# Attention over columns on one core: score blocks from the diagonal on, x transposed from a second layout, factors summed by DMAs

## The chip, the core and the metric

The kernel runs on one core of a Trainium2 chip. The engines that matter here are TensorE (PE, with its weight loads shown apart as PEld), VectorE (DVE), ScalarE (ACT), GpSimd (POOL) and the queues that issue DMAs (SP for all DMAs of the kernel before). The metric is the device time of one execution in microseconds (us); lower is better.

## The reference

Four blocks follow each other on `x` of 8 x 512 x 512 float32 values. Only the first is touched by the change, and the sum of `factors` that the second one uses:

```python
def _L0_attn_ref(x):
    scores = jnp.einsum('bci,bcj->bij', x, x)
    weights = jax.nn.softmax(scores, axis=-1)
    context = jnp.einsum('bij,bcj->bci', weights, x)
    return context
...
x = L0_attn_x
x = x + _layernorm(_L0_attn_ref(_layernorm(x, axis=-1)), axis=-1)
x = x + _layernorm(_L0_ffn_ref(_layernorm(x, axis=-1), L0_ffn_factors, L0_ffn_bias), axis=-1)
```

In the first block each batch's scores are a 512 x 512 matrix that is symmetric, because it is the product of `x` transposed with `x`. The second block multiplies `x` by the sum of eight 512 x 512 factors. Two more blocks (grouped attention, gated FFN) follow.

## The kernel before

`four_blocks` calls one function per block; each ends with all engines meeting, and then the next begins. The change is in `column_attention`. A batch is 4 tiles of 128 rows by 512 columns (`T` = 4, `N` = 512, `P` = 128), and the eight batches `b` are worked on one after the other, with `p` = 0 or 1 as the half of each doubled buffer. Every engine has its own program, and semaphores tie them together; the order in which each engine works is the order in which its program is written.

For one batch the steps are these.

- SP loads `x` of the next batch and one factor.
- DVE takes the statistics of the four tiles (`stats_of`), POOL turns them into scales (`scales_of`, four short instructions of 4 columns), DVE normalises (`xn`, L335) and rounds to the float32r type (`xh`, L341), and POOL forms the rest (`xl` = `xn` - `xh`, L231). A product of two float32 matrices is made of three float32r products: high by high, low by high, high by low.
- PE, `scores` of tile t (S0 to S3 below): 12 matmuls of 128x512 into one PSUM bank of two. Behind each S, `turn` makes 4 transposes of `xn` (128x128 each) into one of two banks `turned`. ACT copies them to `xth` (L292), DVE forms `xtl` (L357).
- DVE takes the row maximum (L345), ACT the exponential into `prob` (L282), DVE the inverse of the sum, POOL multiplies (L236). PE turns `prob` (4 transposes per tile), ACT and DVE make `pth` and `ptl` from it in the same way.
- PE, `contexts` of tile t (C0 to C3): again 12 matmuls of 128x512, for the batch before. DVE takes their statistics, POOL makes the scales, ACT normalises (`normed`, L301), and POOL adds to `x` (L247), one batch later still.
- DVE adds the factor that was loaded to `factor_sum` (L391, 128x2048).

The loops over batches are real loops on the engines except for the first and last batches (`over_batches`, `over_batches_two_behind`). `following.statistics` and `following.row_scales` already do the statistics of batch 0 for the second block.

## Time and profile before

| | us |
|---|---|
| median of three runs | 1650.66 (1650.22 to 1652.57) |
| the profiled execution's own time | 1653.88 |
| its span, from first to last instruction | 1652.0 |
| stage in question: start to the second block's first matmul | 257.05 |

The profile is of one execution. A row names the line, the engine, the instruction with what it writes and reads, and its shape; times of groups are sums, and a mean in nanoseconds. In the timeline the first number is the start in us from the start of the span, the second the length; a count such as x4 behind the shapes says how many instructions were merged into the row; a bracket says how long the engine was idle before it, and what ended that. Matmuls are pipelined, so the time that one costs is the distance between two starts.

### The profile page before, as it was taken

How to read it: one execution, taken by the hardware profiler on the slowest of the kernel's cores; microseconds unless marked ns; L12 is line 12 of the kernel's file. 1: busy time of each engine (PE TensorE's matmuls, PEld its weight loads, DVE VectorE, ACT ScalarE, POOL GpSimd, SP SyncE). 2: the span in 40 equal slices, each digit the busy share in tenths (PEclk: the TensorE clock that was granted, in tenths of full speed). 3: DMA queues.
4: the chain of work that ended last, by engine and by line, in shares of the span. 5: the costliest groups of instructions: out<-in, count | busy, mean ns of one | idle time of the engine just before them, and what ended most of it. 6: DMA issues, size and time to landing. Idle time of an engine off the chain costs nothing.

```text
span 1652.0 us, 22026 instructions
## 1 busy us (share of the span) xinstructions
PE 1498.8 (91%) x7332; PEld 1214.2 (73%) x7332; DVE 1048.3 (63%) x2091; ACT 789.7 (48%) x1506; POOL 733.4 (44%) x914
## 2 busy tenths in 40 slices
PE   4999996995899999999999998579899999999996
PEld 3777775874687877778787876467688888888885
DVE  4698846874888888888888778545424334234233
ACT  1333334644877878687878777321212222222121
POOL 3486742663444545454545445213243333333331
PEclk9999997997999999999999999889999999999998
DMA  4121102224000202020202020222110110100100
GB/s 152 52 102 51 50 1 71 76 89 141 1 1 1 77 1 77 2 77 1 77 1 77 1 96 1 83 96 90 33 51 1 51 51 0 51 32 18 51 26 26
DMA packets 41797, 80.00 MB, mean 48 GB/s; under 512 B 2416, under 2 KB 3440, under 8 KB 41712
## 3 DMA queue, kind: packets, MB, share of 16 engines
q1 hardware_dynamic: 41712, 78.93, 13.7%
q8 instruction: 46, 0.75, 0.2%
q14 instruction: 39, 0.32, 0.1%
HBM read 53.75 MB, written 25.17 MB: 48 GB/s over the span
## 4 chain that ended last, share of the span: by engine, by line
PE 57%; DVE 10%; POOL 4%; issue 3%; ACT 3%; DMA 1%; SPq 0%; POOLq 0%; DVEq 0%; ACTq 0%
PE f_inner L57 22%; PE g_side L1381 12%; PE f_down L1792 9%; PE g_score L57 5%; PE g_turned L1401 5%; DVE g_ptl L1305 2%; PE g_output L1427 2%; PE g_output L1429 2%; DVE g_neg_max L1291 2%; DVE f_wl L1716 1%; POOL g_prob L1016 1%; PE f_inner L1764 1%; POOL g_power L990 1%; DVE g_q L1220 1%; ACT g_pth L1167 1%
## 5 line engine op out<-in xcount | busy, mean ns | idle before, releaser
L1016 POOL TENSOR_SCALAR g_prob<-g_prob,g_inv_sum 128x512 f32<-128x512 f32 x256 | 178.7, 698 | 308.4 <-DVE g_inv_sum L1296 308.4
L57 PE MATMUL f_inner<-f_xth,f_wh 128*128 128x512 f32 x704 | 281.3, 400 | 15.8 <-DVE f_wl L1716 12.7
L57 PE MATMUL f_inner<-f_xtl,f_wh 128*128 128x512 f32 x704 | 279.5, 397 | 0.0
L1685 DVE SCALAR_TENSOR_TENSOR f_hidden<-f_inner,f_inner_scale,f_silu 128x512 f32<-128x512 f32 x88 | 66.0, 750 | 313.8 <-PE f_inner L57 313.8
L1574 POOL TENSOR_TENSOR f_hl<-f_hidden,f_hh 128x512 fp32r<-128x512 f32 x88 | 128.1, 1456 | 296.8 <-DVE f_hh L1691 296.8
L1626 ACT ACTIVATE f_silu<-f_inner,f_inner_scale 128x512 f32<-128x512 f32 x88 | 60.7, 690 | 413.8 <-PE f_inner L57 413.8
L1291 DVE TENSOR_REDUCE g_neg_max<-g_score 128x1 f32<-128x512 f32 x256 | 175.4, 685 | 83.9 <-PE g_score L57 82.7
L1125 ACT ACTIVATE g_prob<-g_score,g_neg_max 128x512 f32<-128x512 f32 x256 | 177.0, 691 | 96.9 <-DVE g_neg_max L1291 94.7
L1305 DVE TENSOR_TENSOR g_ptl<-g_turned,g_pth 128x512 fp32r<-128x512 f32 x256 | 173.8, 679 | 15.6 <-ACT g_pth L1167 13.6
L1401 PE MATMUL g_turned<-identity,g_prob 128*128 128x128 f32 x1024 | 155.2, 274 | 27.1 <-DVE g_ptl L1305 27.0
L57 PEld LDWEIGHTS f_inner<-f_xth,f_wh 128*128 128x128 f32 x704 | 133.1, 189 | 54.6 <-DVE f_wl L1716 17.5
L1167 ACT CAST g_pth<-g_turned 128x512 fp32r<-128x512 f32 x256 | 149.5, 584 | 46.7 <-PE g_turned L1401 44.6
L1401 PEld LDWEIGHTS g_turned<-identity,g_prob 128*128 128x128 f32 x1024 | 121.3, 140 | 64.3 <-issue 34.4
L57 PEld LDWEIGHTS f_inner<-f_xtl,f_wh 128*128 128x128 f32 x704 | 133.2, 189 | 31.7
L1792 PE MATMUL f_down<-f_wh,f_hh 128*128 128x512 f32 x352 | 140.1, 398 | 0.9 <-POOL f_hl L1574 0.9
L1792 PE MATMUL f_down<-f_wh,f_hl 128*128 128x512 f32 x352 | 139.3, 396 | 0.0
L57 PE MATMUL g_score<-g_kh,g_q 128*128 128x512 f32 x256 | 122.2, 478 | 2.7 <-DVE g_q L1220 2.7
L1427 PE MATMUL g_output<-g_pth,g_v 128*128 128x512 f32 x256 | 101.0, 395 | 1.6 <-DVE g_ptl L1305 1.6
L57 PE MATMUL g_score<-g_kl,g_q 128*128 128x512 f32 x256 | 100.9, 394 | 0.0
L1429 PE MATMUL g_output<-g_ptl,g_v 128*128 128x512 f32 x256 | 100.6, 393 | 0.0
L1792 PEld LDWEIGHTS f_down<-f_wh,f_hh 128*128 128x128 f32 x352 | 66.3, 188 | 16.9 <-POOL f_hl L1574 1.3
L1792 PEld LDWEIGHTS f_down<-f_wh,f_hl 128*128 128x128 f32 x352 | 66.4, 189 | 15.5
(200 smaller groups left out, 3460.3 us busy)
## 6 DMA issues: line engine op xcount, KB each, us to landing
x_resident<-x SPq DMA_DIRECT2D x8, 1024.0 KB, 7.0
x_mixed<-x_resident SPq DMA_DIRECT2D x8, 1024.0 KB, 4.4
x_pair<-x_mixed SPq DMA_DIRECT2D x8, 1024.0 KB, 7.8
g_res<-x_mixed SPq DMA_DIRECT2D x8, 1024.0 KB, 6.1
x_attended<-g_res SPq DMA_DIRECT2D x8, 1024.0 KB, 5.1
x_pair<-x_attended SPq DMA_DIRECT2D x8, 1024.0 KB, 5.7
factor<-factors SPq DMA_DIRECT2D x7, 1024.0 KB, 5.2
out<-x_pair SPq DMA_DIRECT2D x7, 1024.0 KB, 4.3
```

Of the source, the lines that this page charges most:

```text
L57: last = nc.tensor.matmul(out, lhsT, rhs, start=(n == 0), stop=(n == len(pairs) - 1))
L1016: nc.gpsimd.tensor_scalar(prob[:, at, :], prob[:, at, :], inv_sum[:, at:at + 1], 1.0, ALU.mult, ALU.mult).then_inc(prob_ready, 1)
L1125: nc.scalar.activation(prob[:, at, :], score[u % 2][:, :], ACT.Exp, bias=neg_max[:, at:at + 1], scale=1.0, accum_out=row_sum[:, at:at + 1] ...
L1167: nc.scalar.copy(pth[:, (turn_u // T) % 2, :, at * P:(at + 1) * P], blocks_of(turned[turn_u % 2][:, :])).then_inc(hi_ready, 1)
L1291: nc.vector.reduce_max(neg_max[:, at:at + 1], score[u % 2][:, :], AX, negate=True).then_inc(max_ready, 1)
L1305: nc.vector.tensor_tensor(ptl[:, at, :, cols], blocks_of(turned[turn_u % 2][:, :]), pth[:, at, :, cols].bitcast(F32), ALU.subtract).then_i ...
L1381: last = nc.tensor.matmul(out[:, bank_cols], *pairs[n], start=(k == 0 and n == 0), stop=(k == T - 1 and n == 2))
L1401: mm = nc.tensor.transpose(turned[turn_u % 2][:, cols], prob[:, turn_u % 4, cols], s.identity[:, :])
L1427: nc.tensor.matmul(output[hd % 2][:, :], lhsT, pth[:, hd % 2, t, :], start=(t == 0), stop=False)
L1429: mm = nc.tensor.matmul(output[hd % 2][:, :], lhsT, ptl[:, hd % 2, t, :], start=False, stop=(t == T - 1))
L1574: nc.gpsimd.tensor_tensor(hl[:, at, :], hidden[:, at, :], hh[:, at, :].bitcast(F32), ALU.subtract).then_inc(hl_ready, 1)
L1792: last = nc.tensor.matmul(down[t][:, :], l[:, at, cols], r[:, i, 2, :], start=(i == 0 and n == 0), stop=(i == IT - 1 and n == len(halves) ...
```

## The change

What it does, step by step.

- **Scores.** Tile t multiplies only the columns from block t on: 12 matmuls of 512, 384, 256 and 128 columns for t = 0 to 3. ACT copies the blocks right of the diagonal out of PSUM into `upper` (`copy_upper`), and PE transposes them into the place of the blocks left of it in the later tiles (1, 2 and 3 transposes for t = 1, 2, 3). The row maximum waits for the copy.
- **x transposed.** It is no longer turned on PE. The host gives `x_t`, the transpose of the raw `x`, as a further input; SP loads it in two halves per batch into `xt`, ACT makes `xth` and DVE `xtl` from SBUF. It is not normalised: since the rows of the weights sum to one, the context of the raw `x` differs from that of the normalised one by a scale and a shift per row, which the layernorm behind takes out. POOL computes the epsilon that goes with it (`raw_eps`, one more instruction per batch).
- **Normalising.** `xn` moves from DVE to POOL, `xh` from DVE to ACT (straight from `x`), `xl` from POOL to DVE.
- **Factors.** Factor 0 is loaded as before. Factors 1 to 7 are added to `factor_sum` in SBUF by DMAs with an add, issued from POOL, each behind a wait for the one before; the DVE instruction L391 goes. At the end of the stage POOL waits for the last one.
- **Output.** The output statistics and scales are made for two tiles at a time (`output_stats`, `output_scales(b, h)`, four instructions per half), `normed` has four buffers, and PE's order is new. All programs of the stage are written out for eight batches, with no loop left.

The core of the diff; the parts removed are in the functions above, and "..." marks what is left out.

```diff
+    def load_x(b):
+        sp.dma_start(s.x[:, b * T:(b + 1) * T, :], rows_of(x_in, b)).then_inc(x_loaded, 16)
+
+    def load_half(b, h):
+        if b > 0:
+            sp.wait_ge(xtl_ready, (b - 1) * T + 2 * h + 2)
+        sp.dma_start(xt[:, 2 * h:2 * h + 2, :],
+                     rows_of(xt_in, b)[:, 2 * h:2 * h + 2, :]).then_inc(xt_loaded[h], 16)
+
+    load_x(0)
+    for b in range(B):
+        if b < B - 1:
+            sp.wait_ge(x_loaded, b * 16 + 16)
+            load_x(b + 1)
+        for h in range(2):
+            load_half(b, h)
+        if b == 0:
+            sp.dma_start(s.factor_sum[:, :, :], rows_of(factors, 0)).then_inc(factor_loaded, 16)
...
     def scales_of(b):
...
+        nc.gpsimd.tensor_scalar(raw_eps[:, b % T, :], mv[:, :, 1], EPS, EPS, ALU.add, ALU.mult)
...
+            nc.gpsimd.tensor_scalar(xn[:, t, :], s.x[:, b * T + t, :], mv[:, t, 0:1], rs[:, t:t + 1],
+                                    ALU.subtract, ALU.mult).then_inc(xn_ready, 1)
...
+        nc.gpsimd.tensor_tensor(ove[:, half], omv[:, half, 1], raw_eps[:, b % T, half], ALU.add)
...
+    def add_factor(b):
+        if b == 1:
+            pool.wait_ge(factor_loaded, 16)
+        else:
+            pool.wait_ge(factor_summed, (b - 1) * 16)
+        nc.gpsimd.dma_start(s.factor_sum[:, :, :], rows_of(factors, b),
+                            accum_op=ALU.add).then_inc(factor_summed, 16)
...
+    normalised(0, range(T))
...
+    def body(b, p, first, last):
+        if b >= 2:
+            add(b - 2, 0)
+            output_scales(b - 2, 1)
+            add(b - 2, 1)
+            add(b - 2, 2)
+        probabilities(b, p, 0)
+        if last:
+            following.row_scales(nc, s, pool)
+        else:
+            scales_of(b + 1)
+        probabilities(b, p, 1)
         if not last:
-            for t in range(T):
-                lo_of(b + 1, 1 - p, t)
-
-    over_batches_two_behind(pool, body)
-    output_scales(B - 2)
-    for t in range(T):
+            normalised(b + 1, (0, 1, 2))
+        probabilities(b, p, 2)
+        if not last:
+            normalised(b + 1, (3,))
+        if not first:
+            output_scales(b - 1, 0)
+        probabilities(b, p, 3)
+        if b >= 2:
+            add(b - 2, 3)
+        if not first:
+            add_factor(b)
...
+        nc.scalar.activation(xh[:, p, t, :], s.x[:, b * T + t, :], ACT.Identity, bias=shift[:, t:t + 1],
+                             scale=rs[:, t:t + 1]).then_inc(xh_ready, 1)
...
+    def copy_upper(b, t):
+        act.wait_ge(scored, b * T + t + 1)
+        nc.scalar.copy(upper[t][:, :], score[t % 2][:, (t + 1) * P:]).then_inc(copied, 1)
...
+        nc.scalar.copy(xth[:, p, t, :], xt[:, t, :]).then_inc(xth_ready, 1)
...
+    def body(b, p, first, last):
+        hi_of_xt(b, p, 0)
+        hi_of_xt(b, p, 1)
+        copy_upper(b, 0)
+        if not first:
+            hi_of_prob(b - 1, 1 - p, 2)
+            hi_of_prob(b - 1, 1 - p, 3)
+        if b >= 2:
+            norm(b - 2, 2)
+        exp(b, p, 0)
+        copy_upper(b, 1)
+        if b >= 2:
+            norm(b - 2, 3)
+        exp(b, p, 1)
+        copy_upper(b, 2)
+        if not last:
+            hi_of_xn(b + 1, 1 - p, 0)
+        exp(b, p, 2)
+        if not last:
+            hi_of_xn(b + 1, 1 - p, 1)
+        hi_of_prob(b, p, 0)
+        if not last:
+            hi_of_xn(b + 1, 1 - p, 2)
+        hi_of_prob(b, p, 1)
+        exp(b, p, 3)
+        if not last:
+            hi_of_xn(b + 1, 1 - p, 3)
+        if not first:
+            norm(b - 1, 0)
+            norm(b - 1, 1)
+        hi_of_xt(b, p, 2)
+        hi_of_xt(b, p, 3)
...
+    def lo_of_xn(b, p, t):
+        dve.wait_ge(xn_ready, b * T + t + 1)
+        dve.wait_ge(xh_ready, b * T + t + 1)
+        nc.vector.tensor_tensor(xl[:, p, t, :], xn[:, t, :], xh[:, p, t, :].bitcast(F32),
+                                ALU.subtract).then_inc(xl_ready, 1)
...
+        nc.vector.tensor_tensor(xtl[:, p, t, :], xt[:, t, :], xth[:, p, t, :].bitcast(F32),
+                                ALU.subtract).then_inc(xtl_ready, 1)
 
     def maximum(b, p, t):
         dve.wait_ge(scored, b * T + t + 1)
+        if t < T - 1:
+            dve.wait_ge(copied, b * (T - 1) + t + 1)
...
     def body(b, p, first, last):
+        if b >= 2:
+            output_stats(b - 2, 3)
         if not last:
...
+            tile_stats(b + 1, 0)
+            tile_stats(b + 1, 1)
+            tile_stats(b + 1, 2)
+        maximum(b, p, 0)
+        if not first:
+            lo_of_prob(b - 1, 1 - p, 2)
+            lo_of_prob(b - 1, 1 - p, 3)
+        if not last:
+            tile_stats(b + 1, 3)
+            stats_of(b + 1)
+        if last:
+            dve.wait_ge(added, T)
+            following.statistics(nc, dve, [s.x[:, t, :] for t in range(T)])
+        inverse(b, p, 0)
+        maximum(b, p, 1)
+        lo_of_xt(b, p, 0)
+        if not first:
+            output_stats(b - 1, 0)
+        inverse(b, p, 1)
+        lo_of_xt(b, p, 1)
+        maximum(b, p, 2)
+        if not last:
+            lo_of_xn(b + 1, 1 - p, 0)
+        inverse(b, p, 2)
+        if not last:
+            lo_of_xn(b + 1, 1 - p, 1)
+        if not first:
+            output_stats(b - 1, 1)
+        lo_of_prob(b, p, 0)
+        maximum(b, p, 3)
+        lo_of_prob(b, p, 1)
+        if not last:
+            lo_of_xn(b + 1, 1 - p, 2)
+        inverse(b, p, 3)
+        if not last:
+            lo_of_xn(b + 1, 1 - p, 3)
+        if not first:
+            output_stats(b - 1, 2)
+        lo_of_xt(b, p, 2)
+        lo_of_xt(b, p, 3)
...
+        if t > 0:
+            pe.wait_ge(copied, b * (T - 1) + t)
+        for r in range(t):
+            nc.tensor.transpose(score[t % 2][:, block_at(r)], upper[r][:, block_at(t - r - 1)],
+                                s.identity[:, :])
+        products(nc, score[t % 2][:, t * P:],
+                 [(l[:, p, k, block_at(t)], r[:, p, k, t * P:])
                   for k in range(T) for l, r in ((xh, xh), (xl, xh), (xh, xl))]).then_inc(scored, 1)
...
     def body(b, p, first, last):
+        scores(b, p, 0, first)
+        if not first:
+            turn(b - 1, 1 - p, 2, b == 1)
+            turn(b - 1, 1 - p, 3, b == 1)
+        scores(b, p, 1, first)
+        if not first:
+            contexts(b - 1, 1 - p, 0)
+        scores(b, p, 2, first)
+        if not first:
+            contexts(b - 1, 1 - p, 1)
+        turn(b, p, 0, first)
+        scores(b, p, 3, first)
+        turn(b, p, 1, first)
+        if not first:
+            contexts(b - 1, 1 - p, 2)
+        if last:
+            turn(b, p, 2, first)
+            turn(b, p, 3, first)
+        if not first:
+            contexts(b - 1, 1 - p, 3)
+
```

PE's program, before, in the steady state: behind the 12 matmuls of S (`score`) stand four transposes of `xn`.

```order
L57 MATMUL score<-xl,xh 128x512
L57 MATMUL score<-xh 128x512
L57 MATMUL score<-xh,xl 128x512
L57 MATMUL score<-xl,xh 128x512
L439 MATMUL turned<-identity,xn 128x128 x4
```

PE's program now, around S3 (the fourth score tile): the turn of `prob`'s tile 0, the three blocks turned from copies, and the first of 12 narrow matmuls.

```order
L57 MATMUL context<-ptl,xth 128x512
L543 MATMUL turned<-identity,prob 128x128 x4
L532 MATMUL score<-identity,upper 128x128 x3
L57 MATMUL score<-xh 128x128
L57 MATMUL score<-xh,xl 128x128
L57 MATMUL score<-xl,xh 128x128
```

The four transposes of `xn` behind each score tile are gone, `turn` serves `prob` alone, and the matmuls of this tile are a quarter as wide.

DVE's program before, in the steady state, from the factor on (REGISTER_ALU is the loop's bookkeeping).

```order
L391 TENSOR_TENSOR factor_sum<-factor_sum,factor 128x2048
L350 RECIPROCAL inv_sum<-row_sum 128x1
L344 REGISTER_ALU
L345 TENSOR_REDUCE neg_max<-score 128x1
L354 REGISTER_ALU
L357 TENSOR_TENSOR xtl<-turned,xth 128x4x128
L335 TENSOR_SCALAR xn<-x_resident,mv,rs 128x512 x2
L350 RECIPROCAL inv_sum<-row_sum 128x1
```

DVE's program now, from the last two tiles of `xtl` of one batch to the work that C0 of that batch waits for (`ptl` of `prob`'s tiles 2 and 3).

```order
L441 BN_STATS obn<-context 128x6
L419 TENSOR_TENSOR xtl<-xt,xth 128x512 x2
L441 BN_STATS obn<-context 128x6
L449 BN_AGGR omv<-obn 128x2 x2
L398 BN_STATS bn<-x_resident 128x6 x3
L426 TENSOR_REDUCE neg_max<-score 128x1
L436 TENSOR_TENSOR ptl<-turned,pth 128x4x128 x2
L398 BN_STATS bn<-x_resident 128x6
```

The factor's addition, `xn` and `xh` have left DVE; `xl` and `xtl` now both read two tiles in SBUF, and nine instructions stand ahead of `ptl`'s last two tiles.

POOL's program now, steady state, from the last step of one batch to the scales of the next but one.

```order
L243 TENSOR_SCALAR prob<-prob,inv_sum 128x512
L259 TENSOR_TENSOR x_resident<-x_resident,normed 128x512
L266 DMA factor_sum<-factors 128x4x512
L259 TENSOR_TENSOR x_resident<-x_resident,normed 128x512
L249 TENSOR_TENSOR ove<-omv,raw_eps 128x2
L250 TENSOR_SCALAR oshift<-omv 128x2
L252 TENSOR_TENSOR ors<-ove,minus_half 128x2
L254 TENSOR_TENSOR oshift<-oshift,ors 128x2
L259 TENSOR_TENSOR x_resident<-x_resident,normed 128x512 x2
L243 TENSOR_SCALAR prob<-prob,inv_sum 128x512
```

Before, POOL had no DMA, and in the place of the four `xn` that it has now (L238) stood the four `xl` (L231). The DMA stands ahead of the second half of the output scales, behind which ACT's program has `norm` and then `exp` of the next batch.

## Rows read from the trace of the kernel before

**Rows 1.** The page of the profile: span, and busy time of each engine.

```profile
span 1652.0 us, 22026 instructions
...
PE 1498.8 (91%) x7332; PEld 1214.2 (73%) x7332; DVE 1048.3 (63%) x2091; ACT 789.7 (48%) x1506; POOL 733.4 (44%) x914
```

**Rows 2.** Windows: busy us (xcount) per engine, granted clock, DMA share, GB/s.

```profile
19.30:44.50 25.20, 18.89 (x80) 15.13 (x80) 14.18 (x32) 7.41 (x16) 10.49 (x12) 0.89 0.24 84
44.50:71.00 26.50, 26.44 (x120) 21.64 (x121) 17.75 (x35) 7.13 (x15) 12.62 (x12) 0.91 0.22 80
```

**Rows 3.** Timeline of PE, steady state, one group of twelve matmuls.

```profile
111.97 0.48 PE L57 MATMUL context<-pth,xth 128*128 128x512 f32 x1
112.29 0.39 PE L57 MATMUL context<-pth,xtl 128*128 128x512 f32 x1
...
114.59 0.39 PE L57 MATMUL context<-ptl,xth 128*128 128x512 f32 x1
115.18 0.48 PE L57 MATMUL context<-pth,xth 128*128 128x512 f32 x1
```

**Rows 4.** Timeline of PE in grouped attention: float32r matmuls of 128 columns.

```profile
398.04 0.28 PE L1381 MATMUL g_side<-g_wvl,g_hth 128*128 128x128 f32 x1
...
399.94 0.28 PE L1381 MATMUL g_side<-g_wvh,g_htl 128*128 128x128 f32 x1
```

**Rows 5.** Timeline of DVE: the factor's addition in two batches.

```profile
108.09 2.28 DVE L391 TENSOR_TENSOR factor_sum<-factor_sum,factor 128x2048 f32<-128x2048 f32 x1
...
134.81 2.28 DVE L391 TENSOR_TENSOR factor_sum<-factor_sum,factor 128x2048 f32<-128x2048 f32 x1
```

**Rows 6.** Timeline of POOL beside it, and the same instruction later.

```profile
107.19 0.70 POOL L236 TENSOR_SCALAR prob<-prob,inv_sum 128x512 f32<-128x512 f32 x1 [5.07 <-DVE inv_sum L350]
...
108.27 2.18 POOL L104 TENSOR_SCALAR shift<-mv 128x4 f32<-128x4 f32 x1
...
127.20 0.23 POOL L104 TENSOR_SCALAR oshift<-omv 128x4 f32<-128x4 f32 x1
```

**Rows 7.** Waits of 40 to 260 us: total, times, longest.

```profile
PE turned L439 <- DVE ptl L357: 5.1, 6, 2.3
```

**Rows 8.** Timeline of the stage's start, all engines.

```profile
7.88 0.50 SPq L212 DMA_DIRECT2D factor_sum<-factors  x1
...
10.41 0.24 POOL L103 TENSOR_SCALAR ve<-mv 128x4 f32<-128x4 f32 x1 [8.84 <-DVE mv L328]
...
12.38 1.91 DVE L335 TENSOR_SCALAR xn<-x_resident,mv,rs 128x512 f32<-128x512 f32 x4 [2.07 <-POOL shift L108]
...
14.71 4.47 POOL L231 TENSOR_TENSOR xl<-xn,xh 128x512 fp32r<-128x512 f32 x2 [2.36 <-DVE xh L341]
...
19.28 0.76 PE L57 MATMUL score<-xh 128*128 128x512 f32 x1 [19.28 <-POOL xl L231]
...
24.54 1.05 PE L439 MATMUL turned<-identity,xn 128*128 128x128 f32 x4
...
44.56 0.79 PE L57 MATMUL score<-xh 128*128 128x512 f32 x1 [3.03 <-POOL xl L231]
```

**Rows 9.** Groups by line, 70 to 202 us.

```profile
L247 POOL TENSOR_TENSOR x_resident<-x_resident,normed 128x512 f32 (+1 forms) x20 | 28.3, 1415 | 0.0
...
L357 DVE TENSOR_TENSOR xtl<-turned,xth 128x512 fp32r<-128x512 f32 x20 | 13.6, 682 | 2.1 <-ACT xth L292 2.1
...
L292 ACT CAST xth<-turned 128x512 fp32r<-128x512 f32 x20 | 11.7, 585 | 20.5 <-PE turned L439 20.4
```

**Rows 10.** The page's DMA issues: count, KB each, us to landing.

```profile
factor<-factors SPq DMA_DIRECT2D x7, 1024.0 KB, 5.2
```

**Rows 11.** Timeline of the stage's end.

```profile
248.50 0.39 PE L57 MATMUL context<-ptl,xth 128*128 128x512 f32 x1
...
252.09 2.99 ACT L301 ACTIVATE normed<-context,oshift,ors 128x512 f32<-128x512 f32 x4 [13.51 <-POOL oshift L108]
...
257.05 1.33 PE L695 MATMUL turned<-identity,xn 128*128 128x128 f32 x5 [8.16 <-ACT xn L574]
```

More of the change, by code:

```diff
@@ L159, in column_attention @@
         prob = sb("prob", [P, T, N])
-        normed = sb("normed", [P, 2, N])
-        factor = sb("factor", [P, T, N])
+        upper = [sb(f"upper{t}", [P, N - (t + 1) * P]) for t in range(T - 1)]
+        normed = sb("normed", [P, 4, N])
         bn = sb("bn", [P, T, 6])
@@ L244, in add @@
-            def add(b, t):
-                pool.wait_ge(ctx_normed, b * T + t + 1 + T)
-                x = tile_of(s.x, b * T + t)
-                nc.gpsimd.tensor_tensor(x, x, normed[:, t % 2, :], ALU.add).then_inc(added, 1)
-            scales_of(0)
-            for t in range(T // 2):
-                lo_of(0, 0, t)
-            pool.sem_inc(xl_ready, T // 2)
-            def body(b, p, before, last):
-                if before == 2:
-                    output_scales(b - 2)
-                for t in range(T):
-                    normalise(b, p, t)
-                    if t == 0 and not last:
-                        scales_of(b + 1)
-                    if before == 2:
-                        add(b - 2, t)
-                if not last:
-                    for t in range(T):
-                        lo_of(b + 1, 1 - p, t)
@@ L304, in body, with hi_of_xt @@
[L304 to L316 removed]
+            def hi_of_xt(b, p, t):
+                if t % 2 == 0:
+                    act.wait_ge(xt_loaded[t // 2], b * 16 + 16)
+                if t == 0 and b >= 2:
+                    act.wait_ge(ctx_ready, (b - 1) * T)
+                nc.scalar.copy(xth[:, p, t, :], xt[:, t, :]).then_inc(xth_ready, 1)
@@ new lines, in hi_of_prob @@
+            def hi_of_prob(b, p, g):
+                act.wait_ge(turn_ready, b * T + g + 1)
+                nc.scalar.copy(pth[:, p, :, block_at(g)], blocks_of(turned[g % 2][:, :])).then_inc(hi_ready, 1)
+            def norm(b, t):
+                act.wait_ge(oscales, b * 2 + t // 2 + 1)
+                if b == B - 1 and t >= 4:
+                    act.wait_ge(last_added, t - 4 + 1)
+                elif b * T + t >= 4:
+                    act.wait_ge(added, b * T + t - 4 + 1)
+                nc.scalar.activation(normed[:, t % 4, :], context[t][:, :], ACT.Identity,
+                                     bias=oshift[:, t:t + 1], scale=ors[:, t:t + 1]).then_inc(ctx_normed, 1)
@@ L360, in output_stats, with lo_of_prob @@
-            def output_stats(b, t):
-                dve.wait_ge(ctx_ready, (b + 1) * T + t + 1)
-                last = nc.vector.bn_stats(obn[:, t, :], context[t][:, :])
-                if t == T - 1:
-                    last.then_inc(own_obn, 1)
-                    wait_alone(dve, s, own_obn, b + 1)
-                    for t in range(T):
+            def lo_of_prob(b, p, g):
+                dve.wait_ge(hi_ready, b * T + g + 1)
+                nc.vector.tensor_tensor(ptl[:, p, :, block_at(g)], blocks_of(turned[g % 2][:, :]),
+                                        pth[:, p, :, block_at(g)].bitcast(F32), ALU.subtract).then_inc(lo_ready, 1)
@@ L403, in _ @@
-            over_batches(dve, body)
-            dve.wait_ge(added, T + 2)
-            following.statistics(nc, dve, [s.x[:, t, :] for t in range(T)])
-            for t in range(T):
-                output_stats(B - 1, t)
-            for t in range(T):
-                dve.wait_ge(ctx_normed, B * T + t + 1)
-                x = tile_of(s.x, (B - 1) * T + t)
-                nc.vector.tensor_tensor(x, x, normed[:, t % 2, :], ALU.add).then_inc(last_added, 1)
+            for t in range(T):
+                tile_stats(0, t)
@@ new lines, in add_last @@
+            def add_last(t):
+                dve.wait_ge(ctx_normed, (B - 1) * T + t + 1)
+                x = s.x[:, (B - 1) * T + t, :]
+                nc.vector.tensor_tensor(x, x, normed[:, t % 4, :], ALU.add).then_inc(last_added, 1)
+            written_out(body)
+            output_stats(B - 2, 3)
+            for t in range(T - 1):
+                output_stats(B - 1, t)
+            add_last(0)
+            add_last(1)
+            output_stats(B - 1, 3)
+            add_last(2)
+            add_last(3)
```

241 lines of the change are left out of this document (97 added, 144 removed).

## The prediction

> **What bounds the stage now.** The page comes first: PE is busy 91% of a span of 1652.0 us [rows 1]. The change touches only what lies ahead of the second block's first matmul, 257.05 us [rows 11]; the rest I take as unchanged. The timeline of PE in the steady state shows starts of 128x512 matmuls 0.230 us apart (10 steps in 2.30 us), and a group of twelve with its four transposes 3.21 us [rows 3]. A batch has eight such groups, 25.7 us. The factor's addition, once per batch, comes back after 26.72 us [rows 5], so PE stands about 1.0 us per batch. The waits name the reason for most of it: `turned` waits for DVE's `ptl`, 5.1 us in 6 times [rows 7]. So PE sets the period of the batches. At both ends it does not: the first matmul starts at 19.28 us behind a chain of DMA, statistics, scales, `xn`, `xh`, `xl`, and batch 1 starts at 44.56 us, after PE has stood for POOL's `xl` [rows 8].
>
> **PE's sum per batch.** A float32r matmul of 128 columns costs 0.112 us (17 steps in 1.90 us) where its columns alone would be a quarter of 0.230, so below some width the cost is flat [rows 4]. No row has 384 or 256 columns. Bounds: by columns 0.172 and 0.115, from above 0.230 each. I take the columns, since 512 columns go by them nearly (0.213 at the full level of 2.4 GHz) and 0.115 is just over the flat cost of [rows 4]. Twelve each: S0 2.76, S1 2.07, S2 1.38, S3 1.34, together 7.55 us in place of 11.0. A group's four transposes cost 3.21 - 12 x 0.230 = 0.45 with the change over to them and back [rows 3], so `prob`'s four turns cost 1.8, and the six blocks of `upper`, in three groups, 1.0 (bounds 0.7 to 1.35). Contexts stay at 11.0. Sum 21.35 us, against 25.7: 3.5 less by narrower scores, 1.8 less by `xn`'s turns, 1.0 more by `upper`. With both unseen widths at their upper bound it would be 12 x (0.058 + 0.115) = 2.1 more.
>
> **What is moved, and whether it hides.** ACT gets 4 passes from SBUF for `xh` (0.75 each as L301 [rows 11]) and three short copies, below 0.585 each [rows 9]; at 20 passes of at most 0.8 and 4 row sums it stays under 18 us. DVE loses the factor (2.28), `xn` and `xh` and gets `xl`: 24 passes of 0.68 [rows 9], about 16.5 us, and some 1.5 of small ones. POOL is the one to watch. Scales: the four small instructions take from 10.41 to 12.38, 1.97 us [rows 8]; with `raw_eps` 2.3. Two halves of output scales 3.9. Four adds at 1.415 [rows 9], 5.7. Four `prob` and four `xn` of 0.70 [rows 6] (`xn` at most as an add), 5.6. That is 17.5 us. The DMA's issue, D, is in no row of POOL: below it 0 (SP's takes 0.50 and hides [rows 8]), above it four passes of 1.415, 5.7, since it names 2048 columns. I take 1.5, nearer to the SP row. On top come holds. While DVE added the factor, two tiles in SBUF, a POOL instruction of 0.23 us took 2.18 [rows 5, 6]: DVE instructions of that kind stop POOL. That was 2.28 us per batch and is now `xl` and `xtl`, 8 x 0.68 = 5.4. So POOL needs 17.5 to 17.5 + 5.4 + 1.5 = 24.4, and with D at its bound 28.6. The holds cost only where POOL has work at that moment; its program waits for `prob` tiles in four places, so I count half: 21.7, close behind PE.
>
> The Trainium skill, "SBUF — State Buffer", section "SBUF: two separate sides", says that the pair of ports is locked for a whole instruction by whichever of the two engines comes first, so that DVE would also wait for POOL. The trace shows only POOL waiting, while DVE takes its 2.28 us each time [rows 5, 6]; what the other direction would give is the second rival. By the Trainium skill, "DMA: Bandwidth & Descriptors", section "Latency and other measured facts", the start of a DMA from POOL costs about 1 us; with that the sum above would be 0.5 us per batch shorter, and no run here shows it.
>
> **The loop behind C0.** PE order makes a second ring: C0, S2, C1, turn, S3, turn take 2.76 + 1.8 + 2.76 + 0.45 + 1.8 + 0.45 = 10.0; from there ACT must do `pth`, `exp`, `xh`, two `normed` and two `xth`, 4.9 at 0.585 to 0.8, then DVE the last `xtl`, output statistics, three statistics of the next batch, the maximum and `ptl` twice, 8 x 0.68 + 0.4 = 5.8. That is 20.7, before the next C0 may start: shorter than PE's 21.35 by 0.6, so two holds are enough to make it the bound. I therefore keep the 1.0 us per batch of standing that [rows 3, 5] give for before: **period 22.35 us** in place of 26.72.
>
> **The start.** Scales end 0.3 later than 12.38 [rows 8]. Then POOL makes four `xn` (2.8) and DVE four `xl` (2.7), ACT's `xh` beside them; one after the other at worst, so S0 starts at 18.2 (15.9 if they overlap wholly) for 19.28. POOL's two `xl` of 4.47 us are gone. S0 runs at the low clock level as now, 5.26 us [rows 8], to 23.5. S1, partly at the low level, with its copy: 27.1. Maximum, `exp` and S2, S3: about 31. Batch 1's four `xn` and `xl` come behind POOL's `prob` 1 at 30.0: 5.5 more, so batch 1 starts at 35.5 for 44.56 (34 to 38). PE stands some 4 us before, as it did for 3.0 us; then the 26.5 us after 44.5 had a mean clock of 0.91, which cost 2.4 us [rows 2], and I keep that.
>
> **Sum.** 35.5 + 2.4 + 7 x 22.35 (156.5) + 0.9 (two turns of batch 7 within its own body) + 11.0 (last contexts) + the end. The end runs from 248.73 to 257.05, 8.3 us [rows 11]; ACT's four `normed` in a row (2.99) become two, and the statistics of half the tiles are done: 6.6. Sum 212.9, that is 44.2 us less than 257.05. The profiled execution took 1653.88, its span 1652.0, the median 1650.66; the gain comes off each: 1609.7 and, for the median, 1606.5. One step of 1 us in the period is 7 us.
>
> Costed at nothing: 8 MB more of loads. Per batch 3 MB, in 22 us, for 2 MB now; a 1 MB DMA lands in 5.2 us [rows 10]. Their cover is a batch's period, and without it each half of `xt` would hold ACT. The DMA that adds must land within a period, or POOL waits in front of the next; below 22 us it costs nothing, and the last is issued some 20 us before the stage ends. The written out programs cost nothing, as the first batch and the last are that already.
>
> **Rivals.**
> - POOL binds. All holds count and D is 1.5 to 5.7: period 24.4 to 28.6, typically 25. For it: 8 holds for one. Against it: POOL is idle at several waits. It gives 1606.5 + 7 x 2.65 = 1625. Chance 0.25.
> - DVE is held by POOL too. Eight instructions wait half an instruction of 0.7 to 1.4, 0.5 us each; five of them lie in the ring behind C0 or what feeds it: 20.7 + 2.5 = 23.2, so 1612. It is the mechanism of the rule of the Trainium skill ("SBUF — State Buffer") above. Chance 0.2.
> - Narrow matmuls cost more than their columns, up to 2.1 per batch: at most 1621, more likely 1612. [rows 4] speak against a great excess. Chance 0.07.
> - Slower than before: the DMA with its addition (issue on POOL or landing) takes longer than a period. The wait in `add_factor` then stands in front of POOL's next `x` add, output scales, ACT's `normed` and `exp`. It decides from a period of 22.35 + 44.2/7 = 28.7 us; at 30 us it gives 1660. A plain DMA lands in 5.2 [rows 10]. Chance 0.04.
> - The forecast, period 21.35 to 23, 1599 to 1611: chance 0.41. The last 0.03 is for a better start and PE without any standing, below 1599.
>
> **Numbers.** The likeliest is 1606. The range holds the first three rivals in their usual sizes: 1596 (period 21.35, batch 1 at 34 and S0 at 16) to 1628 (period 25.4). What can be told from no change is 0.2%, 3.3 us. Faster needs a period below 28.2: all cases but the slow one and the far end of the first rival. Faster 0.94, within 0.2% 0.02, slower 0.04.
>
> **What the profile after would show.** PE: distances of 0.172, 0.115 and 0.112 us within S1, S2, S3; a period (from S0 to S0) of 22.35; first matmul near 18, batch 1 at 35.5; the second block's first matmul at 213. POOL: if its idle time in the steady state is near nothing, and PE waits for `xl`, `turned` or `context` with POOL behind, the first rival holds; if `xl` and `xtl` of DVE take over 0.68, the second; if `x_resident` on POOL waits for a DMA, the slow one. I would be wrong above all through D and through how many holds hit.

## The result, and the profile after

The changed kernel took 1661.13 us (median of four runs, 1659.48 to 1663.25), the kernel before 1650.62 beside it (1650.22 to 1652.57). The ratio is 1.0062, with a 95% interval of 1.0045 to 1.0079: slower by 0.6%, where 1606 was forecast. Run again later, the ratio was 1.0052 (1.0034 to 1.0069).

The page of the changed kernel first, beside [rows 1]:

```profile
span 1657.7 us, 21618 instructions
...
PE 1470.7 (89%) x7252; PEld 1196.0 (72%) x7252; DVE 1023.0 (62%) x2050; ACT 818.5 (49%) x1562; POOL 774.5 (47%) x963
```

PE's busy time is 28 us less, and the span is longer. So PE waits more. POOL is busy 41 us more than before. One line of its code stands out: 32 `xn` take 78 us, 2.45 in the mean, where 0.70 each, as I had counted, gives 22. This is the answer for line 238 of the changed kernel, `xn` on POOL (min, median and max in ns):

```profile
L238 POOL TENSOR_SCALAR xn<-x_resident,mv,rs x32: 2066/2600/2613, 12.5 to 211.2; 128x512 f32<-128x512 f32 x32
...
who waited for it (us, times):
  DVE xl L414: 44.5, 25
```

The prediction has 0.70 us for it. The start shows what that does, against [rows 8] (timelines of the changed kernel):

```profile
12.50 9.86 POOL L238 TENSOR_SCALAR xn<-x_resident,mv,rs 128x512 f32<-128x512 f32 x4
...
23.23 0.77 PE L57 MATMUL score<-xh 128*128 128x512 f32 x1 [23.23 <-DVE xl L414]
...
46.11 0.77 PE L57 MATMUL score<-xh 128*128 128x512 f32 x1 [9.64 <-issue]
```

Four `xn` take 9.86 us where 2.8 was counted; S0 starts at 23.23 (19.28 before) and batch 1 at 46.11 (44.56 before). In the steady state a batch looks like this on PE, POOL and ACT (timelines, from one S0 to the next):

```profile
98.40 0.47 PE L57 MATMUL score<-xh 128*128 128x512 f32 x1 [0.18 <-issue]
...
109.70 0.75 PE L57 MATMUL context<-pth,xth 128*128 128x512 f32 x1 [3.75 <-issue]
...
127.59 0.47 PE L57 MATMUL score<-xh 128*128 128x512 f32 x1 [0.88 <-issue]
```

```profile
116.23 7.28 POOL L238 TENSOR_SCALAR xn<-x_resident,mv,rs 128x512 f32<-128x512 f32 x3
123.50 0.68 POOL L243 TENSOR_SCALAR prob<-prob,inv_sum 128x512 f32<-128x512 f32 x1
124.17 2.60 POOL L238 TENSOR_SCALAR xn<-x_resident,mv,rs 128x512 f32<-128x512 f32 x1
126.74 0.19 POOL L249 TENSOR_TENSOR ove<-omv,raw_eps 128x2 f32<-128x2 f32 x1
```

```profile
128.71 1.45 ACT L345 ACTIVATE normed<-context,oshift,ors 128x512 f32<-128x512 f32 x2 [3.48 <-POOL oshift L254]
```

This period is 29.19 us, against 26.72 in [rows 5]; over the steady state of this trace a batch takes 27.8 to 29.2. Read from POOL on: `prob` of tile 2 stands behind three `xn` (DVE had its `inv_sum` at 119.13, and `prob` starts at 123.50), the output scales behind the fourth (`omv` was there at 122.54, and they start at 126.74). ACT waits 3.48 us for those scales, and its `xth` stand behind `normed`. In DVE's program the last `xtl` waits for `xth`, and behind it stand statistics, a maximum and the last two `ptl`, without a gap. PE's first context group needs `xtl` and `ptl`; the `ptl` come last, and end where its wait of 3.75 us ends:

```profile
108.33 1.28 DVE L436 TENSOR_TENSOR ptl<-turned,pth 128x512 fp32r<-128x512 f32 x2
```

This is the ring of "The loop behind C0" in the prediction, with POOL's `xn` now in front of ACT's `normed`. The wait costs PE once more: in the stretch behind it (109.70 to 112.81) the granted clock is 0.50, the lower of its two levels (1.2 GHz), and the matmuls of this group start 0.43 us apart for 0.23. That is 1.7 us of the period. The windows put POOL's sum beside it:

```profile
98.40:127.59 29.19, 23.30 (x118) 19.46 (x119) 18.53 (x37) 13.97 (x27) 24.48 (x26) 0.94 0.41 108
```

POOL is busy 24.48 us of the period. My sum of 17.5 with 2.45 in place of 0.70 for each of four `xn` gives 24.5. The issue of the DMA (1.35 us) is not in that column; with it POOL has 25.8 us of work.

The prediction also asked whether DVE is held by POOL. It is. In the same timeline:

```profile
101.35 1.35 POOL L266 DMA_DIRECT2D factor_sum<-factors  x1
101.50 3.67 DVE L419 TENSOR_TENSOR xtl<-xt,xth 128x512 fp32r<-128x512 f32 x2 [2.59 <-ACT xth L333]
102.26 1.74 POOL L259 TENSOR_TENSOR x_resident<-x_resident,normed 128x512 f32<-128x512 f32 x1
```

Two `xtl` take 3.67 us, where two of 0.68 each would take 1.4. How much of that is the add's and how much the DMA's, the kernels without the DMA show below.

### The profile page after: what moved, and what is told of

Read it like the earlier page. It is cut to its first block, busy times and chain, and to the rows that moved or that the text cites. A ratio compares the mean times of both kernels' runs of the same rounds, so it can differ in the third digit from the quotient of the medians.

```text
span 1657.7 us, 21618 instructions
## 1 busy us (share of the span) xinstructions
PE 1470.7 (89%) x7252; PEld 1196.0 (72%) x7252; DVE 1023.0 (62%) x2050; ACT 818.5 (49%) x1562; POOL 774.5 (47%) x963
## 3 DMA queue, kind: packets, MB, share of 16 engines
q1 hardware_dynamic: 42368, 79.98, 13.9%
## 4 chain that ended last, share of the span: by engine, by line
PE 59%; DVE 10%; POOL 3%; issue 3%; ACT 2%; DMA 1%; SPq 0%; POOLq 0%; DVEq 0%; ACTq 0%
PE f_inner L57 22%; PE g_side L1497 13%; PE f_down L1908 9%; PE g_score L57 5%; PE g_turned L1517 5%; PE g_output L1543 2%; PE g_output L1545 2%; DVE g_ptl L1421 2%; DVE g_neg_max L1407 2%; DVE f_wl L1832 1%; DVE g_q L1336 1%; PE f_inner L1880 1%; POOL g_prob L1132 1%; DVE f_hidden L1801 1%; POOL g_power L1106 1%
## 5 line engine op out<-in xcount | busy, mean ns | idle before, releaser
L1421 DVE TENSOR_TENSOR g_ptl<-g_turned,g_pth 128x512 fp32r<-128x512 f32 x256 | 173.6, 678 | 15.5 <-ACT g_pth L1283 13.5
L57 PE MATMUL score<-xh 128*128 128x512 f32 (+3 forms) x128 | 45.6, 356 | 37.5 <-DVE xl L414 23.2
```

What stands on the lines that cost most here:

```text
L57: last = nc.tensor.matmul(out, lhsT, rhs, start=(n == 0), stop=(n == len(pairs) - 1))
L1421: nc.vector.tensor_tensor(ptl[:, at, :, cols], blocks_of(turned[turn_u % 2][:, :]), pth[:, at, :, cols].bitcast(F32), ALU.subtract).then_i ...
```

## The experiments

The theory: the form of POOL's `xn`, that is the pair of operations it is written with, costs the forecast gain. The main rival: the DMA that adds does, by its issue on POOL and by what it holds on DVE. A smaller question is which of the forecast's other terms stand once the first is mended.

The runs were made in three groups, each beside the kernel before, with medians of 1651.87, 1652.19 and 1652.5 us (1650.62 beside the result). So a difference of times between two groups is uncertain by one or two us; where it matters, the stage's time in the traces stands beside it. "The stage" is the time from the start of the span to the second block's first matmul: 257.05 before, 259.24 in the changed kernel.

### The form of POOL's `xn`, alone

```diff
-nc.gpsimd.tensor_scalar(xn[:, t, :], s.x[:, b * T + t, :], mv[:, t, 0:1], rs[:, t:t + 1],
-                        ALU.subtract, ALU.mult).then_inc(xn_ready, 1)
+nc.gpsimd.tensor_scalar(xn[:, t, :], s.x[:, b * T + t, :], rs[:, t:t + 1], shift[:, t:t + 1],
+                        ALU.mult, ALU.add).then_inc(xn_ready, 1)
```

> The changed kernel, with one edit: POOL's xn is x * rs + shift (multiply, add) instead of (x - mean) * rs (subtract, multiply). Theory A, the form of POOL's xn is the cause: in the changed kernel these 32 instructions took 2.45 us each, while grouped attention's instruction of the same shape with two column operands and multiply, add (g_xn) took 0.77. xn then takes about 0.77, a batch loses up to 4 x 1.68 = 6.7 us of the 29.2 us from S0 to S0, down to about 22.5 us, batch 1 starts some 13 us earlier than 46 us, and the median is near 1661 - 47 - 13 = 1601 us, at least below 1615. Theory B, the port that DVE and POOL share and the DMA's issue are the cause, xn's 2.45 us being mostly time held back: xn stays above 1.5 us and the median above 1640 us.

Measured: 1611.57 us (1609.64 to 1612.66), ratio 0.9749 (0.9736 to 0.9763). That is 49.6 us less than the changed kernel, by one line that computes the same function from `shift`, which POOL had made already; the stage ends at 210.17 for 259.24. It is within theory A's bound of 1615, though 10 us above its likeliest 1601, and theory B (above 1640) falls. Line 238 and the start in its trace:

```profile
L238 POOL TENSOR_SCALAR xn<-x_resident,rs,shift x32: 760/768/1312, 12.6 to 163.1; 128x512 f32<-128x512 f32 x32
```

```profile
12.64 4.59 POOL L238 TENSOR_SCALAR xn<-x_resident,rs,shift 128x512 f32<-128x512 f32 x4
...
18.11 0.76 PE L57 MATMUL score<-xh 128*128 128x512 f32 x1 [18.11 <-DVE xl L414]
...
36.84 0.77 PE L57 MATMUL score<-xh 128*128 128x512 f32 x1 [5.31 <-issue]
```

```profile
100.00:122.00 22.00, 21.09 (x119) 18.25 (x118) 19.44 (x37) 14.01 (x28) 18.22 (x27) 1.00 0.57 144
```

The period is 22.15 us (DVE's statistics of a batch start at 83.89, 106.04 and 128.19), PE is busy 21.09 of 22 us, POOL 18.22 without the DMA's issue, and the granted clock is 1.00. This is the kernel that the prediction describes.

### `xn` back on DVE

```diff
+            def xn_of(b, t):
+                if t == 0:
+                    dve.wait_ge(scales, b + 1)
...
+                nc.vector.tensor_scalar(xn[:, t, :], s.x[:, b * T + t, :], mv[:, t, 0:1], rs[:, t:t + 1],
+                                        ALU.subtract, ALU.mult).then_inc(xn_ready, 1)
+
             def lo_of_xn(b, p, t):
+                xn_of(b, t)
```

> The changed kernel, with xn given back to DVE, directly ahead of each xl; POOL has no xn. Theory A: POOL loses 4 x 2.45 us per batch and is no bound any more; DVE gains 4 x 0.5 to 1.2 us and is near 21 us per batch, so the period is 22 to 24 us and the median 1600 to 1618 us. Theory B: with xn gone from POOL the instructions held back are others, and the median stays above 1635 us.

`normalised` and its calls on POOL are gone (not shown). Measured: 1613.87 us (1612.91 to 1615.44), ratio 0.9763 (0.9748 to 0.9778), with a period of 22.92, as theory A has it. The same subtraction and multiplication takes DVE 0.533 us, so it is dear on POOL and not on DVE, and either cure gives the gain.

### Four forms in one kernel

```diff
+                    dst, src, m, r = xn[:, t, :], s.x[:, b * T + t, :], mv[:, t, 0:1], rs[:, t:t + 1]
+                    if t == 0:
+                        done = nc.gpsimd.tensor_scalar(dst, src, m, r, ALU.subtract, ALU.mult)
+                    elif t == 1:
+                        done = nc.gpsimd.tensor_scalar(dst, src, m, r, ALU.add, ALU.mult)
+                    elif t == 2:
+                        done = nc.gpsimd.tensor_scalar(dst, src, r, m, ALU.mult, ALU.subtract)
+                    else:
+                        done = nc.gpsimd.tensor_scalar(dst, src, r, m, ALU.mult, ALU.add)
```

> The changed kernel, with POOL's xn in four forms, one for each tile, same operands in shape and place: subtract, multiply; add, multiply; multiply, subtract; multiply, add. The values of xn are then not those of the reference in three of four tiles. Theory A says that the duration goes with the pair of operations, and this run says with which part of it: if subtraction is what is slow, tiles 0 and 2 take 2.0 to 2.6 us and the others 0.77; if it is any pair that doesn't begin with a multiplication, tiles 0 and 1; if only multiply, add is fast, tiles 0, 1 and 2. Theory B, time held back by DVE: all four alike, since the same DVE work stands beside them.

The values of three tiles in four are not the reference's here; only durations are read. Measured: 1645.13 us in the one run, period 27.5. The first batch (timeline of POOL and DVE; a form per line):

```profile
12.66 2.09 POOL L240 TENSOR_SCALAR xn<-x_resident,mv,rs 128x512 f32<-128x512 f32 x1
14.74 1.30 POOL L242 TENSOR_SCALAR xn<-x_resident,mv,rs 128x512 f32<-128x512 f32 x1
14.79 0.69 DVE L422 TENSOR_TENSOR xl<-xn,xh 128x512 fp32r<-128x512 f32 x1 [4.43 <-POOL xn L240]
...
16.03 2.62 POOL L244 TENSOR_SCALAR xn<-x_resident,rs,mv 128x512 f32<-128x512 f32 x1
...
18.63 1.30 POOL L246 TENSOR_SCALAR xn<-x_resident,rs,mv 128x512 f32<-128x512 f32 x1
```

The forms with a subtraction cost 2.09 and 2.62 us, those with an addition 1.30: not all four alike, so theory B falls here too. Tiles 1 to 3 run while DVE forms the `xl` of the tile before (14.79), and are held by it: 0.76 alone against 1.30 beside an `xl`, and 2.07 against 2.60 in the changed kernel, are the same 0.53 us. That the `xl` is what holds them is read from their standing side by side. Freed of it, a subtraction costs 2.07, an addition 0.76, in either place of the pair.

### Four more forms

```diff
+                    if t == 0:
+                        done = nc.gpsimd.tensor_scalar(dst, src, m, None, ALU.subtract)
+                    elif t == 1:
+                        done = nc.gpsimd.tensor_scalar(dst, src, 0.5, 2.0, ALU.subtract, ALU.mult)
+                    elif t == 2:
+                        done = nc.gpsimd.tensor_scalar(dst, src, m, None, ALU.add)
+                    else:
+                        done = nc.gpsimd.tensor_scalar(dst, src, 0.5, 2.0, ALU.add, ALU.mult)
```

> The changed kernel with xn of the four tiles in four other forms on lines of their own, which change the values of xn: tile 0 subtracts a column and does no more, tile 1 subtracts 0.5 and multiplies by 2, tile 2 adds a column and does no more, tile 3 adds 0.5 and multiplies by 2. Theory A (a subtraction of a scalar operand is what is slow on POOL): tiles 0 and 1 at least 2.0 us when not held, tiles 2 and 3 below 0.8. Rival 1 (two operations with two different column operands are slow when one is a subtraction): tile 1 is fast, 0.7 to 0.8. Rival 2 (it is slow only with two operations): tile 0 is fast. No theory of the whole time; two slow tiles would give about 1645, four fast ones 1612.

Here too the kernel computes other values. Measured: 1622.09 us in the one run. The lines are tiles 0 to 3 in this order, with min, median and max in ns:

```profile
L240 POOL TENSOR_SCALAR xn<-x_resident,mv x8: 1568/1576/1587, 12.4 to 171.4; 128x512 f32<-128x512 f32 x8
L242 POOL TENSOR_SCALAR xn<-x_resident x8: 1924/1932/1935, 13.9 to 173.0; 128x512 f32<-128x512 f32 x8
L244 POOL TENSOR_SCALAR xn<-x_resident,mv x8: 1573/1579/2112, 15.9 to 174.9; 128x512 f32<-128x512 f32 x8
L246 POOL TENSOR_SCALAR xn<-x_resident x8: 613/618/627, 17.9 to 177.1; 128x512 f32<-128x512 f32 x8
```

Subtracting 0.5 and multiplying by 2 takes 1.93 us, adding 0.5 and multiplying by 2 takes 0.62: rival 1 falls, the columns are not the reason. Subtracting a column and doing no more takes 1.58, so rival 2 falls. But adding a column and doing no more takes 1.58 us, as long as subtracting it, so theory A is too narrow as well: it held for tiles 0, 1 and 3 only up to its number (1.58 for "at least 2.0") and not for tile 2. What these rows bear out is that POOL has a few cheap pairs (multiply with multiply, add with multiply, multiply with add: 0.62 to 0.77 us) and that what is outside them costs 1.6 to 2.1. Why stays open.

### One slow tile in four

The kernel with the cheap form, but tile 3 subtracts and multiplies as in the change.

```diff
+                    if t == 3:
+                        nc.gpsimd.tensor_scalar(xn[:, t, :], s.x[:, b * T + t, :], mv[:, t, 0:1], rs[:, t:t + 1],
+                                                ALU.subtract, ALU.mult).then_inc(xn_ready, 1)
```

> The kernel e1_mult_add with the xn of one tile in four (tile 3) in the form of the changed kernel, subtraction and multiplication. POOL is busy 18.2 of 22 us per batch in e1, and gets 1.3 to 1.8 more. Theory A (POOL's idle 3.8 us take it, PE stays the bound): period 22.15 to 22.5, time 1611 to 1614. Theory B (POOL's work between two prob tiles stands in the ring whatever POOL's idle time elsewhere): period 23.0 to 24.0, time 1618 to 1626. The two slow tiles of e2_forms gave a period of 27.5.

Measured: 1619.45 us (1618.56 to 1620.54), ratio 0.9799 (0.9781 to 0.9816), 7.9 us above the kernel with four cheap tiles; period 23.3, with one of 24.6. Theory B: POOL had 3.8 us per batch in which it wasn't busy (2.4 without the DMA's issue), and still passes on 1.2 of its extra 1.3. The tile stands between two `prob` tiles and in front of output scales; that this is why POOL's idle time elsewhere doesn't take it is the theory's reading, and no run moved the tile.

Five kernels now differ in nothing but POOL's `xn`. Per batch it takes POOL 3.6, 4.9, 5.7, 7.3 and 9.8 us in the steady state, and the times are 1611.6, 1619.5, 1622.1, 1645.1 and 1661.1 us: the more of the one, the more of the other, though not in proportion.

### The DMA that adds, left out: in the changed kernel, and in the one with the cheap form

```diff
-                if not first:
-                    add_factor(b)
```

> The changed kernel without the seven DMAs that add the factors 1 to 7 (that part of the sum is left out). Theory A: the DMA's issue is 1.35 us on POOL, which is the bound, so the period falls by 1.0 to 1.9 us from 29.2 and the median by 7 to 13 us, to 1648 to 1654. A rival for which the DMA is the main cause (issue, its hold on the port, or its landing of 9.7 us): the median falls by over 30 us, below 1630.

> The kernel e1_mult_add without the seven DMAs that add (factors 1 to 7 are left out of the sum). Theory A (PE sets the period, the DMA's 1.36 us of issue on POOL and what it holds on DVE lie beside it): the period stays within 0.3 us of 22.15, the time is 1609 to 1612. Theory B (the ring behind the first context group is the bound, as its wait of 0.9 us in e1 says): the DVE instructions of xtl fall from 1.35 to 0.7 to 0.9 us each, the period falls by 0.8 to 1.2 us, and the time is 1603 to 1606. In the changed kernel the same cut gave 11.7 us.

Both kernels leave factors 1 to 7 out of the sum. Measured: 1649.4 us (1646.34 to 1651.66), 11.7 less than the changed kernel, ratio 0.9981 (0.9972 to 0.999); and 1605.55 us (1604.0 to 1608.81), 6.0 less than with the cheap form, ratio 0.9722 (0.97 to 0.9743). The stage ends at 246.31 in the first (12.9 less) and at 204.00 in the second (6.2 less). The first settles the main rival: were the DMA the main cause, leaving it out would have taken off over 30 us. The time is in theory A's range; a batch takes 26.4 us, once 27.6, where it had 27.3 to 28.2. In the second, theory B holds in time and period:

```profile
100.00:144.00 44.00, 43.92 (x245) 37.94 (x244) 38.82 (x74) 28.86 (x56) 36.40 (x51) 1.00 0.30 96
```

The period is 21.2 and PE is busy 43.92 of 44 us, so in the kernel with the cheap form it was still the ring and not PE that set the 22.15. `xtl` fell from 1.354 to 1.094 us, less than theory B had it (0.7 to 0.9); two of them now take 2.74 us beside two of POOL's adds.

### The same DMA elsewhere in POOL's order

```diff
                 if b >= 2:
                     add(b - 2, 0)
+                    add_factor(b)
                     output_scales(b - 2, 1)
...
-                if not first:
-                    add_factor(b)
```

> The kernel e1_mult_add with the DMA that adds moved in POOL's order: not behind the add of tile 3, where its issue (1.37 us at 124.11) fell together with two xtl of DVE that took 3.72 us, but behind the add of tile 0, in front of the output scales, where POOL stood 1.53 us for omv. Nothing is left out. Theory A (what the DMA costs is that its issue holds xtl, whose last one the context group waits for): POOL's idle time hides the issue, two xtl take 2.4 us or less, the period falls from 22.15 towards the 21.2 of the kernel without the DMA, the time is 1605 to 1608. Theory B (POOL's 1.37 us cost the same wherever they stand, or the issue now delays the output scales by as much): period 22 to 22.3, time 1610 to 1613.

Measured: 1606.63 us (1603.03 to 1606.97), ratio 0.9715 (0.9696 to 0.9734), period 21.2. It is the fastest kernel of this study that does all the work. In its timeline the issue begins when POOL's add has ended, 0.6 us before the second `xtl` ends, and goes on beside statistics:

```profile
100.46 2.75 DVE L420 TENSOR_TENSOR xtl<-xt,xth 128x512 fp32r<-128x512 f32 x2
100.93 1.74 POOL L259 TENSOR_TENSOR x_resident<-x_resident,normed 128x512 f32<-128x512 f32 x1
102.61 1.37 POOL L266 DMA_DIRECT2D factor_sum<-factors  x1
103.14 0.68 DVE L442 BATCH_NORM_STATS2 obn<-context 128x6 f32<-128x512 f32 x1
103.86 0.25 DVE L450 BATCH_NORM_AGGREGATE omv<-obn 128x2 f32<-128x6 f32 x2
...
104.20 0.19 POOL L249 TENSOR_TENSOR ove<-omv,raw_eps 128x2 f32<-128x2 f32 x1 [0.22 <-DVE omv L450]
```

The two `xtl` take 2.75 us, as in the kernel without the DMA, for 3.72 with the issue ahead of the add. So the issue, where it stood, held DVE for 1.0 us, and the statistics, which read one tile, keep their 0.68 beside it. POOL's wait for `omv` shrinks to 0.22, so its own 1.37 us are hidden too. Theory A holds, and 4.9 of the DMA's 6.0 us come back (4.8 of 6.2 in the stage). The DMA lands later there, 13.5 us for 10.0, still within a period.

### Full squares of scores again, with the cheap form

```diff
-                for r in range(t):
-                    nc.tensor.transpose(score[t % 2][:, block_at(r)], upper[r][:, block_at(t - r - 1)],
-                                        s.identity[:, :])
-                products(nc, score[t % 2][:, t * P:],
-                         [(l[:, p, k, block_at(t)], r[:, p, k, t * P:])
+                products(nc, score[t % 2][:, :],
+                         [(l[:, p, k, block_at(t)], r[:, p, k, :])
```

> The kernel e1_mult_add with the scores as full squares again: twelve matmuls of 512 columns for each of the four tiles, no copies from the diagonal's right, no turned blocks. Nothing is left out of the result. Theory A (PE sets the period of e1, 22.15 us): the narrower matmuls, seen 0.175, 0.120 and 0.113 us apart in e1, save 12 x (0.055 + 0.110 + 0.117) = 3.4 us per batch against 0.230, and six turned blocks cost 0.9; without both the period is 2.5 longer, 24.6, and the time is 1611.6 + 8 x 2.5 = 1631 (1627 to 1634). Theory B (the ring through POOL, ACT and DVE is as long as PE's sum, and the copies stand in it): the period is 23 to 23.8, and the time is 1617 to 1625.

The copies into `upper` and the waits for them are gone too (not shown). Measured: 1624.35 us (1623.45 to 1624.7), ratio 0.9828 (0.9811 to 0.9846). The time falls under theory B (1617 to 1625), the period of 24.43 under theory A (24.6), and the stage ends at 226.33 for 210.17, 16.2 us later. The span is 13.9 longer, because the blocks behind the stage took 2.2 us less in this trace (1396.5 for 1398.7), which leads to the next runs. Theory A's premise, that PE alone sets the 22.15, the kernel without the DMA has already corrected; PE is busy 21.24 of 22.15 us there, and 23.88 of 24.41 here, so in both it is near the bound and not quite it. The narrower scores are worth 2.3 us per batch net of the copies.

### Both kernels once more

> The changed kernel once more, word for word, beside the kernel before. The question is what of its 10.5 us lies in the changed stage. Its first trace reaches the second block's first matmul at 259.24 us, 2.2 later than before, and needs 1398.5 us from there to the end, where before needed 1394.9; the difference sits near the end of the third block, where the granted clock was 0.90 for 0.96. Theory A (the 3.5 us behind the stage are the clock's, and come and go between executions): a second trace gives 259 to 260 us again and 1394 to 1399 for the rest. Theory B (the stage itself varies by as much): the second block starts more than 1.5 us away from 259.2. The time should be 1658 to 1664 by both.

> The kernel before once more, word for word, for a second trace. Theory A (the stage's time repeats, the rest varies with the clock): the second block's first matmul at 257 us within 1 us, the rest 1392 to 1399 us. Theory B: the stage varies by over 1.5 us.

Measured: 1662.14 us (1658.52 to 1663.5) for the changed kernel; 1652.21 for before. The stage ends at 261.43 and 255.21. For the changed kernel that is theory B (2.2 us from the first trace; its batches now take 28.3 to 30.1 us each), for before 1.8 us less, also B by the bound of 1.5. The blocks behind the stage took 1394.9 and 1395.2 us in the two traces of before, and 1398.5 and 1398.9 in those of the changed kernel, though their program is the same. That repeats, so theory A's "come and go" does not show in these four traces; what comes and goes in them is the stage, by 2 us. The windows show what is with it, 750 to 800 us behind the stage, for the changed kernel (first trace) and for before (second trace), PE first and the granted clock third from the end:

```profile
1009.24:1059.24 50.00, 39.40 (x180) 30.15 (x179) 34.04 (x74) 24.67 (x53) 26.84 (x36) 0.90 0.13 43
```

```profile
1005.21:1055.21 50.00, 39.37 (x191) 30.24 (x190) 35.40 (x76) 24.47 (x53) 27.08 (x36) 0.97 0.12 43
```

The same work meets a granted clock of 0.90 in the one and 0.97 in the other. In the second trace of the changed kernel this stretch has 0.97 and two earlier ones 0.98 instead of 1.00. So of the 10 us by which the changed kernel is slower, 2 to 6 lie in the stage (259.24 and 261.43 for 257.05 and 255.21), and some 3.6 behind it, where the clock dips at other places. The two first traces differ by 5.7 us in span, the two second by 9.9. Two traces each don't settle more: fifteen executions of the kernel before lie between 1650.8 and 1655.4 us, with a mean granted clock of 0.972 at the short end and 0.968 at the long one, and neither end was traced. Why the dips move with the program ahead of them was not tested.

## Why the prediction was wrong

**The failed step** is in "What is moved, and whether it hides": "Four `prob` and four `xn` of 0.70 [rows 6] (`xn` at most as an add), 5.6." I took `prob`'s row, a multiplication with a multiplication, for another pair of operations with the same shape, and then drew an upper bound (1.415) from an instruction with two tiles. Neither bounds it: `xn` costs 2.07 us alone and 2.45 in the mean, holds by `xl` included. I had made a bound for D, the other unseen price, and none from the operation here. The trace of before has no subtraction with multiplication of this shape on POOL; it has a multiplication with addition by two columns (`g_xn`, L1030), at 0.77 us, and I didn't write `xn` in that form. 7.0 us per batch were missing from POOL's sum, 5.5 of them without any hold. With 2.07 and D the sum is 24.3 us, above PE's 21.35 before a hold is counted, and with 2.45 it is 25.9: by my own sums the first rival would have been the forecast. The one-line edit that gives `xn` a price near the assumed one (0.77 alone, 0.90 in the steady state) takes 49.6 us off, of the 55 by which the result lies above the forecast. So this step is the cause of the miss, but for some 5 us.

**The steps that held**, seen in the kernel with the cheap form:

- PE's sum of 21.35 us: 21.2 where nothing else binds (DMA left out, or moved). The starts of matmuls of 384 columns are 0.175 us apart, those of 256 columns 0.120, those of 128 columns 0.113; taken were 0.172, 0.115 and 0.112.
- The period of 22.35: 22.15, but by luck, for the reason was not the one given. It was part of the second rival, DVE held by POOL, and not the 1.0 us of standing carried over from before. That rival's price of 0.5 us per instruction was near (`xtl` 1.35 for 0.68, `xl` 0.90), its place in the ring right, but only part of it decided: it had a period of 23.2. Its 1612 is met by the 1611.57 in number only.
- D of 1.5: 1.36. It lands in 9.7 us (page of the changed kernel), within a period, so the slow rival's wait never came. The result is slower all the same, and not by that rival's mechanism.
- S0 at 18.2, batch 1 at 35.5, the second block at 212.9: 18.11, 36.84 and 210.2. Batch 1 is 1.3 us later and the end 2.7 us earlier, so errors in part offset each other.
- "The rest I take as unchanged" held for the program and not for the time: it took 3.8 us longer (1398.7). With the 2.7 us that the stage is shorter, the span is 1608.9, where the same sum gave 1607.8 (1652.0 less 44.2). Most of what is left between 1606.5 and 1611.6 is how the profiled executions lay against their medians: before 3.2 us above (1653.88 for 1650.66), this one 0.9 below (1610.71 for 1611.57).

**The rivals.** "POOL binds" named the right engine and place, and its far end (28.6) is close to the 29.2 seen, but it was reached there by full holds and a D of 5.7, neither of which is what happened: D is 1.36, and POOL still stood at some waits (24.48 busy and 1.35 of issue in 29.19). The range ended at 1628, since the far end was given no weight. Its lower end is a slip: a period of 21.35 and batch 1 at 34 give 1606.5 - 7.0 - 1.5 = 1598, not 1596; nothing hangs on it.

The Trainium skill, "SBUF — State Buffer", section "SBUF: two separate sides", has the two engines exclude each other. The prediction weighed it against [rows 5, 6], where only POOL is seen waiting, and let it be a rival. The runs agree with the rule in this direction: two `xtl` take 2.75 us beside POOL's add, and one after the other they and the add would take 2.7 (1.4 and 1.3). A DMA's issue ahead of the add made it 3.67.

## What to carry to other kernels

A price read from a row is that of its operation pair, not only of its engine and shape: before work is moved to POOL, find a row there with the same two operations, or write the work in a form that has one. Where an engine's sum comes out within a few us of the bound, its least certain price can decide the forecast and needs an upper end of its own. Try a DMA that POOL issues at a place where DVE does work that reads one tile; here that was worth 5 us.

## What the runs showed of the hardware that was not expected

- POOL on a 128x512 float32 tile: subtract with multiply 2.07 us, multiply with subtract 2.62 beside an `xl`, subtract or add a column alone 1.58, subtract with multiply by constants 1.93; add with multiply and multiply with add 0.76, add with multiply by constants 0.62. DVE does the first in 0.533.
- POOL's cheap `xn` beside one DVE `xl` takes 1.30 for 0.76 us, and DVE's `xtl` beside a POOL add and a DMA's issue 1.8 each for 0.68: each engine is held beside the other.
- The issue of a 1 MB DMA with addition occupies POOL for 1.36 us, held a pair of DVE's `xtl` for 1.0 where it stood beside them, and lands after 9.7 to 13.5 us; a plain one landed after 5.2 [rows 10].
- Blocks whose program was not changed took 1394.9 and 1395.2 us behind the kernel before and 1398.5 and 1398.9 behind the changed one (two traces each), with dips of the granted clock in other places.
